# Cross attention on one core: scores of two head groups issued together, Strassen's blocks in three PSUM banks instead of four

## What is computed

```python
k, v = ctx @ Wk.T + bk, ctx @ Wv.T + bv          # 25088 x 512 each
q = layernorm(x) @ Wq.T + bq                     # 256 x 512
x = x + softmax(q @ k.T / 8) @ v                 # per head, 8 heads of 64
```

## Time and profile before

| | |
|---|---|
| time before, median of 3 runs | 1519.84 us (1518.81 to 1520.62) |
| the profiled execution | 1517.86 us, of which 1516.1 us are the profile's span |
| PE busy | 1452.8 us (96% of the span) |
| DVE busy | 1298.2 us (86%) |
| ACT busy | 1254.2 us (83%) |
| POOL busy | 951.0 us (63%) |
| share of the chain that ended last | PE 85%, DVE 6%, DMA 3%, ACT 2%, POOL 2% |

### The profile page before, as it was taken

One profiled execution on the slowest core, in us unless ns is written; L12 is line 12 of the kernel. 1 busy time (PEld: TensorE's weight loads), 2 busy tenths in 40 slices (PEclk: granted clock), 3 DMA queues, 4 the chain that ended last, 5 costly groups with the idle time before them and its releaser, 6 DMA issues.

```text
span 1516.1 us, 47982 instructions
## 1 busy us (share of the span) xinstructions
PE 1452.8 (96%) x17942; PEld 1206.2 (80%) x17942; DVE 1298.2 (86%) x1768; ACT 1254.2 (83%) x3039; POOL 951.0 (63%) x980
## 2 busy tenths in 40 slices
PE   6999999999999999999999999999999887599999
PEld 5788888888888888888888888888888764377776
DVE  6788989888888888898888888888889887788995
ACT  4788888888888888888888888888988875666883
POOL 6586877778687878787777878787878522500000
PEclk9999999999999999999999999999999998699999
DMA  4357555565656565655556565656566578766991
GB/s 187 71 110 143 115 135 133 122 138 117 143 113 139 111 143 112 139 119 134 135 116 143 113 145 111 138 111 145 112 137 130 116 154 223 175 232 241 337 329 46
DMA packets 460175, 220.40 MB, mean 145 GB/s; under 512 B 433856, under 2 KB 440000, under 8 KB 453328
## 3 DMA queue, kind: packets, MB, share of 16 engines
q1 hardware_dynamic: 459680, 218.22, 59.6%
q10 hardware_dynamic: 432, 1.32, 0.3%
HBM read 111.96 MB, written 0.56 MB: 74 GB/s over the span
## 4 chain that ended last, share of the span: by engine, by line
PE 85%; DVE 6%; DMA 3%; ACT 2%; POOL 2%; issue 1%; SPq 0%; DVEq 0%; ACTq 0%; POOLq 0%
PE ps_proj L1626 55%; PE ps_s L1676 9%; PE ps_o L1694 8%; PE ps_proj L1895 6%; PE ps_o L1911 3%; DMA pt_s<-p_s 2%; DVE wsp L1375 2%; PE ps_proj L1655 1%; POOL ctx_s L580 1%; DVE cmax L1163 1%; DVE p_s L1176 1%; PE ps_proj L1911 1%; DMA ctx_f<-ctxt_dram 1%; ACT prob L815 0%; PE ps_o L1596 0%
## 5 line engine op out<-in xcount | busy, mean ns | idle before, releaser
L1626 PE MATMUL ps_proj<-ctx_s,wk_s 128*128 128x256 f16 x4032 | 480.6, 273 | 3.9 <-ACT ps_proj L769 3.6
L1626 PE MATMUL ps_proj<-wv_s,ctx_s 128*128 128x256 f16 x4032 | 480.6, 273 | 1.5 <-ACT ps_proj L771 1.5
L580 POOL TENSOR_TENSOR ctx_s<-t_f,ctx_s 128x512 f16<-128x512 f32 x192 | 265.0, 1390 | 279.9 <-ACT ctx_s L717 279.9
L1626 PEld LDWEIGHTS ps_proj<-ctx_s,wk_s 128*128 128x128 f16 x4032 | 379.9, 98 | 66.4 <-issue 24.3
L1626 PEld LDWEIGHTS ps_proj<-wv_s,ctx_s 128*128 128x128 f16 x4032 | 379.9, 98 | 63.4 <-issue 11.4
L815 ACT ACTIVATE prob<-ps_s,nmax 128x256 f32<-128x256 f32 x776 | 357.1, 476 | 8.3 <-DVE nmax L1170 8.1
L1163 DVE TENSOR_REDUCE cmax<-ps_s 128x4 f32<-128x1024 f32 x194 | 237.5, 1224 | 123.9 <-PE ps_s L1676 123.9
L1176 DVE SCALAR_TENSOR_TENSOR p_s<-prob,p_s 128x1024 f16<-128x1024 f32 x196 | 320.3, 1634 | 0.7 <-ACT p_s L826 0.7
L580 POOL TENSOR_TENSOR ctx_s<-ctx_f,ctx_s 128x512 f16<-128x512 f32 x144 | 215.7, 1498 | 10.3 <-ACT ctx_s L712 5.4
L826 ACT ACTIVATE p_s<-prob 128x1024 f16<-128x1024 f32 x196 | 206.6, 1054 | 6.7
L1694 PE MATMUL ps_o<-v_s,pt_s 128*128 128x64 f16 x4704 | 171.6, 194 | 15.2 <-DMA pt_s<-p_s 15.2
(11 more groups left out here) (235 smaller groups left out, 1800.4 us busy)
## 6 DMA issues: line engine op xcount, KB each, us to landing
ctx_f<-ctxt_dram SPq DMA_DIRECT2D x48, 1024.0 KB, 5.4
wst<-w_dram SPq DMA_DIRECT2D x96, 512.0 KB, 5.5
pt_s<-p_s SPq DMA_TRANSPOSE x408, 3.1
tisa<-tisa_scores SPq DMA_DIRECT2D x12, 256.0 KB, 5.7
w_in_f<-w_in_dram SPq DMA_DIRECT2D x2, 1024.0 KB, 6.2
w_f<-wk_dram SPq DMA_DIRECT2D x2, 512.0 KB, 6.4
ctx_f<-ctxt_dram SPq DMA_DIRECT2D x2, 512.0 KB, 7.8
w_f<-wv_dram SPq DMA_DIRECT2D x1, 1024.0 KB, 11.3
```

The costliest lines, as they stand in the source:

```text
L580: pool.tensor_tensor(out=low[:, n, :, :], in0=sources[n], in1=high[:, n, :, :], op=ALU.subtract).then_inc(ctx_low, 1)
L1626: ins = pe.matmul(ps_proj[:, bank(h, role), sub * QUARTER:(sub + 1) * QUARTER], lhsT, rhs, start=(fresh and sub == 0 and t == 0 and i == 0 ...
```

## The change

Each half step's two groups of scores are issued back to back, ahead of all units, each in two banks of its own (`ps_s` for an even group, `ps_o` for an odd one). The output product moves from `ps_o` to one bank, `ps_proj` 3. M5 moves to the bank of C12 and C22 moves to SBUF (`c22_f`). The orders on ACT and DVE are rewritten to go with that: `p_highs` and `p_lows` of a half step's second group now stand in the same half step and no longer in the next.

```diff
+        c22_f = sb("c22_f", [P, 2, QUARTER], F32, cross)
...
-        M1, M5, M6, M2, M7, M3, M4 = (0, 0, 0), (3, 3, 3), (4, 4, 1), (1, 1, 0), (5, 5, 1), (6, 2, 2), (2, 6, 1)
+        M1, M5, M6, M2, M7, M3, M4 = (0, 0, 0), (3, 3, 2), (4, 4, 1), (1, 1, 0), (5, 5, 1), (6, 2, 2), (2, 6, 1)
...
     ACT step:
-                    if strassen:
-                        seed(c + 1, h)
-                    pc, pg = back(c, 2 * h, 1)
-                    if exists(pc, 0):
-                        p_highs(pc, pg)
                     if exists(c, -1) and h == 0:
                         alphas(c - 1, 1)
                     if exists(c, 0) and h == 1:
                         alphas(c, 0)
                     if strassen:
+                        seed(c + 1, h)
+                    if exists(c, 2):
+                        ctx_highs(c + 2, odd, h)
+                    if strassen:
                         copy_m5(c + 1, h)
                     if exists(c, 0):
                         exps(c, 2 * h, odd)
+                        p_highs(c, 2 * h)
+                    if exists(c, 2):
+                        sum_highs(c + 2, odd, h)
                     if exists(c, 0):
-                        p_highs(c, 2 * h)
+                        exps(c, 2 * h + 1, odd)
                     if strassen:
                         block_highs(c + 1, h, C11, 1 - odd)
-                    if exists(c, 2):
-                        ctx_highs(c + 2, odd, h)
                     if exists(c, 0):
-                        exps(c, 2 * h + 1, odd)
+                        p_highs(c, 2 * h + 1)
                     if strassen:
                         for which in (C22, C12):
                             block_highs(c + 1, h, which, 1 - odd)
...
     DVE:
-                dve.tensor_tensor(half_bank(bank(h, 3)), half_bank(bank(h, 1)), m5_f[:, :, :], ALU.add).then_inc(c22_done, 1)
+                dve.tensor_tensor(c22_f[:, :, :], half_bank(bank(h, 1)), m5_f[:, :, :], ALU.add).then_inc(c22_done, 1)
...
     DVE step:
-                    if exists(c, 0):
-                        maxima(c, 2 * h, odd)
-                    pc, pg = back(c, 2 * h, 1)
-                    if exists(pc, 0):
-                        p_lows(pc, pg)
-                    if strassen:
-                        add_u4(c + 1, h)
                     if exists(c, -1):
                         add_o(c - 1, h)
                     if exists(c, 0):
+                        maxima(c, 2 * h, odd)
                         maxima(c, 2 * h + 1, odd)
+                    if strassen:
+                        add_u4(c + 1, h)
+                    if exists(c, 0):
+                        p_lows(c, 2 * h)
                     if strassen:
                         add_c22(c + 1, h)
                         block_lows(c + 1, h, C11, 1 - odd)
                     if exists(c, 0):
-                        p_lows(c, 2 * h)
+                        p_lows(c, 2 * h + 1)
...
     PE:
                 elif m == M5:
-                    pe.wait_ge(block_low, 4 * g - 2 + (2 if isinstance(k, int) and g == 2 else 0))
+                    pe.wait_ge(block_low, 4 * g)
...
-                    pe.wait_ge(block_low, 8 * c + 4)
+                    pe.wait_ge(block_low, 8 if isinstance(c, int) and c == 0 else 8 * c + 4)
...
-                    for half, before, between, behind in ((0, (M1,), (M5, M6), (M2,)), (1, (), (M7, M3), (M4,))):
...
+                    if exists(c, 0):
+                        scores(c, 2 * h, odd)
+                        scores(c, 2 * h + 1, odd)
+                    units(M1, M5, M6)
+                    weighted(0)
+                    units(M2)
+                    weighted(1)
+                    units(M7, M3, M4)
```

More of the change, by code:

```diff
@@ L399, in out_v @@
             return v_s[odd][kk][:, 2 * j:2 * j + 2, i * QUARTER:(i + 1) * QUARTER]
-        C11, C22, C12, C21 = (0, 0, 0), (3, 1, 1), (2, 0, 1), (1, 1, 0)
+        C11, C22, C12, C21 = (0, 0, 0), (None, 1, 1), (2, 0, 1), (1, 1, 0)
         def half_bank(n):
@@ L779, in copy_m5 @@
                     act.wait_ge(c22_done, g - 2)
-                act.activation(m5_f[:, :, :], half_bank(bank(h, 3)), ACT.Copy).then_inc(m5_done, 1)
+                act.activation(m5_f[:, :, :], half_bank(bank(h, 2)), ACT.Copy).then_inc(m5_done, 1)
             def block_highs(k, h, which, odd):
                 role, i, j = which
-                g, ps = 2 * k + h, half_bank(bank(h, role))
+                g, ps = 2 * k + h, c22_f[:, :, :] if which == C22 else half_bank(bank(h, role))
                 if which == C22:
@@ L1161, in maxima @@
                 dve.wait_ge(s_done, NG * c + g + 1)
[L1162 to L1163 removed]
+                dve.tensor_reduce(cmax[:, g % 2, :], score_banks(c, g).rearrange("p b (r k) -> p (b r) k", r=2), AX,
                                   ALU.max).then_inc(cmax_done, 1)
@@ L1218, in add_o @@
                 acc = o_acc[:, half, :, :, :].rearrange("p u r d -> p (u r d)")
-                dve.tensor_tensor(acc, acc, ps_o[:, half, :], ALU.add).then_inc(added, 1)
+                dve.tensor_tensor(acc, acc, out_bank(c, half), ALU.add).then_inc(added, 1)
             def by_rows(t, half):
```

62 lines of the change are left out of this document (31 added, 31 removed).

## The result

The changed kernel takes 1588.19 us (median of 4 runs, 1585.61 to 1589.43) against 1519.32 us for the kernel before (4 runs, 1517.58 to 1520.62): ratio 1.0452, 95% interval 1.0434 to 1.047. It is slower, as predicted, but by 69 us where 125 were forecast; 1588 lies in the range of 1575 to 1695, near its lower end.

The account below looks back on a forecast made before the run. PE bounded the kernel before; after it, M5's loop through ACT and DVE: V half 13.1 + K half 14.2 = 27.3 us a step. 48 x (27.3 - 24.6) = 130 us on 1517.86 gave 1648, stated as 1645; range 1575 to 1695.

Parts of the forecast that it names:

- The bound and the gain on PE: PE bounds the kernel before; one way in and out of scores less cuts a half step from 12.30 to 12.11 us.
- The loop: M5 waits for C21's low part, and so through ACT and DVE for M5 of the half step before.
- The floor: The M5-to-M5 loop with each link at its shortest: K half 12.78, V half 12.57, 25.35 us a step.
- What the floor leaves out: Waits between DVE and POOL, and for `alphas`, raise the V half to 13.1 and the K half to 14.2 us.
- the walk: M5's loop followed link by link with waits on POOL: 27.3 us a step, +130 us; chance 0.50 (1615 to 1690).
- locks in the mean only: Rival: `p_lows` costs its mean of 1.634 us, nothing else waits: 26.2 a step, +77 us, 1595; chance 0.27.
- every C22 waits a full POOL instruction: Rival: C22's low part waits 1.16 us in place of 0.2: +221 us, 1739; chance 0.09 (above 1690).
- The bare loop: Rival: DVE and POOL never meet, so a step takes 25.35 us: +36 us, 1554; chance 0.08.
- PE's order alone decides: Rival: M5's wait is met before PE gets there, PE stays full at 12.11 us: 1500 us; chance 0.04.
- start and end taken as 0: First scores and last chunk move one or two us each, against each other, so they add 0.
- What was to be seen: Signs in the profile after: PE idle before M5 by DVE's low parts, M5 to M5 13 to 14 us, PE about 88%.
- The stall of M7 and M4: On PE in the K half: some 0.7 us, for `add_u4` and `add_c22` behind `nmax`, costing nothing.

Follow-up runs that it names:

- e3_extra_in_loop: Changed kernel plus one needless DVE maximum over 128x512 ahead of C22's low part in each half step: 1709.68 us, ratio 1.1266 to the kernel before.
- e1_low_behind_c21: Changed kernel with only the second `p_lows` on DVE moved back behind C21's low part, into the next half step: 1694.81 us, ratio 1.1161 to the kernel before.
- e6: Changed kernel with `alphas` behind `copy_m5` on ACT and the first group's `maxima` ahead of `add_o` on DVE: 1588.6 us, ratio 1.0466 to the kernel before.
- e10: Opened-loop kernel with the TISA arguments moved ahead of `p_lows`, plus `add_c22` ahead of the first `p_lows` on DVE: 1535.55 us, ratio 1.0121 to the kernel before.
- e2_loop_opened: Changed kernel with second `p_highs` and `p_lows` back in the next half step, both `maxima` and the second v product moved: 1524.97 us, ratio 1.005.

## Why the prediction was right or wrong

**The bound and the gain on PE: right.** 24 scores in 1.42 us, and in the opened loop a V half of 12.09 against 12.11. In the changed kernel the step without M5's waits is 24.17, so the gain is there too (0.43 a step, 0.38 forecast), but as M5 is bound by the loop, it only makes PE wait longer.

**The loop: right in kind.** M5 waits for C21's low part in every regular half step, the same DVE instruction costs 121 us in the loop and nothing off it, and opening the loop gives back 61 us. The floor was a good one. In the V half 12.57 was forecast without waits and the half took 12.65, with 0.14 of it for `p_lows` (1.27 to the next start, not 1.13), so the links themselves were 0.06 shorter than in my sum. In the K half, 12.78 plus the waits measured below gives 13.53, and 13.36 was measured: 0.17 shorter, 0.12 of it at the end (C12 and C21's low parts to M5, 1.33 where I had 1.45).

**The step that failed: "What the floor leaves out", the sizes of the waits on POOL.**

| wait | predicted | measured |
|---|---|---|
| V half, second `p_lows` | 0.3 | 0.14 |
| V half, C22's low part | 0.25 | 0 |
| K half, first `exps` (`alphas`, `nmax`) | 0.65 | 0.43 |
| K half, second `p_lows` | 0.65 | 0.32 |
| K half, C22's low part | 0.15 | 0 |
| sum | 2.0 | 0.89 |

Of the difference between 27.3 and 26.01 us a step (48 x 1.29 = 62 us) these waits are 1.11 and the shorter links 0.23, together 1.34; the walk's own sum before rounding is 27.35, so nothing else is missing. Two reasons. First, C22's low part, which I gave a wait of 0.25 and 0.15, has none. The short instruction of POOL does go first, as the walk has it, but it costs nothing: in the changed kernel C22's low part takes 682 to 687 ns in all 85 instances between 100 and 1200 us, and in all 85 it is an update of `l_acc` that waits and ends 0.14 us after C22's low part has started. The Trainium skill (SBUF — State Buffer, "Who interferes with whom") says that two such instructions contend and that issue order decides who blocks. The traces agree on both: C22's low part takes 1.37 to 1.55 us where POOL's large instruction has started ahead of it (e3_extra_in_loop, e1_low_behind_c21), and `rescale`, which starts 0.10 behind it, is the one that waits in the changed kernel. The walk's example of a wait was read a little wrong as well: the `p_lows` at 620.36 is not issued while POOL is in its sum L564 but 0.03 ahead of its start at 620.39. Second, times between 0 and 1.1 us that depend on where a POOL instruction ends can't be summed from a trace in which everything lies elsewhere: e6 shows a 0.40 us gain on one link returned in full by the next, and e10 a difference of 0.08 us in `nmax`'s lead that costs it 1.13.

**The rival "locks in the mean only"** (1595) came nearest in number, but not by its mechanism: it had no wait but `p_lows`, at 1.634, and `p_lows` took 1.396 in the mean while `nmax` cost 0.49 in the K half. The rival "every C22 waits a full POOL instruction" was the opposite of what happened in the changed kernel; where something stands between the two, a part of it happens in most of the runs (0.25 to 0.87 of the 1.16). "The bare loop" needed the two engines never to meet. "PE's order alone decides" failed where the prediction said: the loop never falls below 12.11 a half step, and only with the loop opened does a V half take 12.09.

**What the prediction did not have.** The arguments of TISA stand inside the loop for one chunk, ahead of C21's low part; taking them out was worth 4.2 us in the opened loop, where I tested it. In the changed kernel the two half steps of that chunk last 19.35 and 16.77 us (scores to scores), some 10 us more than others. The kernel before has irregular places too: between the first scores and those of the last chunk, all that is above 48 regular steps adds up to 12 us in the changed kernel and 10 in the kernel before. So start and end taken as 0 is right to within some 2 us, but by two sums that cancel.

**What was to be seen**: M5 waits by DVE's low parts, yes, 1.11 and 0.38 where 1 to 2 was said; M5 to M5 13.36 and 12.65 where 13 to 14 was said; C22's low part 0.68 always; `nmax` in K halves 0.65; PE at 92%, not 88%. The stall of M7 and M4 of 0.7 us in the K half, which was to cost nothing, did not come: in the regular steps PE waits for nothing but M5's low parts.

## What to carry to other kernels

When a change adds a wait, follow it once round: if the releaser's chain leads back to the waiting instruction, the time of that ring at its shortest is a floor for the step, whatever the engines' sums of work say, and it can be read from the trace within 1 to 2%. Test it by putting one needless instruction in the ring and one beside it. What lies above the floor from two engines that take turns is no constant: it follows from which instruction starts first, jumps by a whole instruction for a shift of 0.1 us, and should go into the range with both signs, not into the sum. To shorten a ring, look at where the operation goes that is taken out of a link: moved on DVE alone, `p_lows` stood in the way of the next link and cost 107 us more (e1_low_behind_c21); moved on ACT and DVE together, with three more moves, the loop opened (e2_loop_opened). No run tells which of them were needed.
